# TensorE's unit loop written out, and the second tile's scores cut in two around half of the output products

## The reference, cut to what matters

```python
for i in range(DEPTH):                                # 6
    x = attn_layer(shift_tokens(x), Wqkv[i], ...) + x
    x = ffn_layer(shift_tokens(x), ...) + x

def attn_layer(x, Wqkv, qs, ksc, Wo):                 # 16 heads of 64, INNER = 1024
    q, k, v = jnp.split(x @ Wqkv, 3, -1)
    q = l2norm(q) * qs;  k = l2norm(k) * ksc          # per head
    q = q * cos * scale + rotate_half(q) * sin * scale
    k = k * cos / scale + rotate_half(k) * sin / scale
    # windows of 32 queries see their own 32 keys and the 32 before them
    attn = jax.nn.softmax(jnp.where(mask, low, q @ k.T * 8.0), -1)
    return (attn @ v) @ Wo

def ffn_layer(x, g, bln, W1, b1, W2, b2):
    xn = layernorm(x) * g + bln
    a, gate = jnp.split(xn @ W1 + b1, 2, -1)
    return a * gelu(gate) @ W2 + b2
```

## Time and profile before

| | us |
|---|---|
| median of 3 runs | 3477.61 |
| lowest, highest | 3473.73, 3481.7 |
| the profiled execution's own time | 3467.71 |
| its span | 3465.9 |
| mean granted TensorE clock | 0.979 of full |

### The profile page before, as it was taken

How to read it: one execution, slowest core, us unless ns; L and a number is a source line. 1 busy time by engine, 2 the same in 40 slices (tenths; PEclk the granted TensorE clock), 3 DMA queues, 4 the chain that set the end, 5 groups by cost and what they waited for, 6 DMA issues and landing times.

```text
span 3465.9 us, 129619 instructions
## 1 busy us (share of the span) xinstructions
PE 3224.8 (93%) x51488; PEld 2289.5 (66%) x51488; DVE 2896.2 (84%) x5656; ACT 2801.5 (81%) x5313; POOL 2685.9 (77%) x1798
## 2 busy tenths in 40 slices
PE   8999799899999899998999999999999999998996
PEld 5777466666666666675667766666766677766665
DVE  6999788788888888897779898888988788887784
ACT  5777588778888788887889888888988788887884
POOL 1001598778888889998789998889988889988883
PEclk9999899999999999999999999999999999999998
DMA  2000011111211111211112211112211112211111
GB/s 66 0 0 0 7 34 37 37 29 39 59 38 39 39 28 51 57 39 35 31 34 53 50 38 38 39 34 55 50 35 39 39 31 54 51 39 33 33 39 51
DMA packets 127341, 129.59 MB, mean 37 GB/s; under 512 B 62380, under 2 KB 75824, under 8 KB 126832
## 3 DMA queue, kind: packets, MB, share of 16 engines
q1 hardware_dynamic: 123232, 112.38, 13.3%
q10 hardware_dynamic: 3600, 9.50, 0.9%
HBM read 19.04 MB, written 2.10 MB: 6 GB/s over the span
## 4 chain that ended last, share of the span: by engine, by line
PE 75%; issue 10%; DVE 6%; POOL 5%; SPq 1%; DMA 1%; ACT 1%; DVEq 0%; POOLq 0%; ACTq 0%
PE ps L1313 23%; PE ps L1335 9%; PE ps L1328 8%; PE ps L1344 7%; PE ps L1357 7%; PE ps L1305 6%; PE ps L1367 4%; PE ps L1169 3%; POOL area L446 2%; PE ps L1161 2%; POOL AQb L453 2%; PE ps L1158 2%; DVE area L991 2%; PE ps L1181 1%; PE ps L1154 1%
## 5 line engine op out<-in xcount | busy, mean ns | idle before, releaser
L1313 PE MATMUL ps<-Wqkv,xsT 128*128 128x512 f32 x2304 | 1138.3, 617 | 9.0 <-DMA Wqkv<-ffn_Wqkv 3.4
L446 POOL TENSOR_TENSOR area<-area,tab 128x512 f32<-128x512 f32 x768 | 960.6, 1280 | 108.8 <-ACT area L634 107.7
L1313 PEld LDWEIGHTS ps<-Wqkv,xsT 128*128 128x128 f32 x2304 | 403.9, 196 | 341.1 <-issue 240.3
L468 POOL TENSOR_TENSOR area<-area,lsum 128x1024 f32<-128x1024 f32 x192 | 365.7, 1905 | 284.9 <-DVE lsum L932 284.8
L453 POOL TENSOR_TENSOR area<-area 128x1024 f32<-128x1024 f32 x192 | 452.8, 2374 | 46.8 <-DVE area L991 46.8
L634 ACT ACTIVATE area<-ps 128x512 f32<-128x512 f32 x768 | 455.1, 593 | 35.2 <-PE ps L1313 34.4
L453 POOL TENSOR_TENSOR AQb<-AQb,area 128x1024 f32<-128x1024 f32 x192 | 449.5, 2364 | 0.1
L639 ACT ACTIVATE area<-area 128x1024 f32<-128x1024 f32 x384 | 396.5, 1065 | 0.1
L1335 PE MATMUL ps<-Wo,area 128*128 128x128 f32 x3072 | 376.4, 281 | 20.9 <-issue 20.8
L1335 PEld LDWEIGHTS ps<-Wo,area 128*128 128x128 f32 x3072 | 356.4, 194 | 33.8 <-issue 25.4
L1328 PEld LDWEIGHTS ps<-BD,area 64*64 64x64 f32 x12288 | 270.0, 133 | 144.8 <-issue 133.4
(11 more groups left out here) (124 smaller groups left out, 6416.3 us busy)
## 6 DMA issues: line engine op xcount, KB each, us to landing
BD<-area SPq DMA_DIRECT2D x1440, 64.0 KB, 2.0
Wqkv<-ffn_Wqkv ACTq DMA_DIRECT2D x12, 512.0 KB, 3.9
x2s<-x2s SPq DMA_DIRECT2D x96, 56.0 KB, 2.1
Wo<-ffn_Wo SPq DMA_DIRECT2D x6, 512.0 KB, 4.9
Wqkv<-ffn_Wqkv ACTq DMA_DIRECT2D x12, 256.0 KB, 3.1
W<-ffn_W SPq DMA_DIRECT2D x6, 341.0 KB
x2s<-x2s SPq DMA_DIRECT2D x96, 7.5 KB, 2.5
x2s<-x2s SPq DMA_DIRECT2D x96, 0.2 KB, 1.9
```

The source lines that it names most:

```text
L446: pool.tensor_tensor(b4[:, :, here], q4[:, :, there], s4[:, :, here], ALU.mult).then_inc((s_bq, s_bk)[j], 1)
L468: pool.tensor_tensor(p3, p3, lsum[:, 1, :].unsqueeze(2).broadcast_to([P, HEADS, 2 * WIN]), ALU.mult).then_inc(s_pn, 1)
L1313: mm(home(kind + part), xsT[:, par, t * P:(t + 1) * P], Wqkv[:, w0:w0 + 512], start=True, stop=True).then_inc(done, 1)
```

## The change

`stack_steps_straight` calls `step` for all 99 steps with plain numbers, and TensorE alone uses it. TensorE's program then has no loop in the stack, no register instructions for its waits, and the static steps' waits in every step. The other four engines keep their loops. Second, `scores(n-1, 1)` is called in two parts: pairs 0 to 3, then `output(n-2, 0, 0)` and `output(n-2, 1, 0)`, then pairs 4 to 7, then the g = 1 products. The waits stand ahead of the first part, and `s_sc` is raised after the second.

```diff
+        def stack_steps_straight(step, lags):
+
+            for n in range(UNITS + lags):
+                u = n % SEQS
+                step(n, u, u % 2, live(n), n // SEQS)
...
-            def scores(n, t):
+            def scores(n, t, pairs=range(PAIRS)):
 
-                need_apart(pe, i_pe, s_mk, 4 * n + 2 * t + 2)
-                if isinstance(n, int):
-                    need_apart(pe, i_pe, s_te, nth(n, EVICTED, "q11" if t else "q00"))
-                for c in range(PAIRS):
+                if 0 in pairs:
+                    need_apart(pe, i_pe, s_mk, 4 * n + 2 * t + 2)
+                    if isinstance(n, int):
+                        need_apart(pe, i_pe, s_te, nth(n, EVICTED, "q11" if t else "q00"))
+                for c in pairs:
...
-                last.then_inc(s_sc, 1)
+                if PAIRS - 1 in pairs:
+                    last.then_inc(s_sc, 1)
...
                 if one:
-                    scores(n - 1, 1)
+                    scores(n - 1, 1, range(0, PAIRS // 2))
...
                     output(n - 2, 0, 0)
                     output(n - 2, 1, 0)
+                if one:
+                    scores(n - 1, 1, range(PAIRS // 2, PAIRS))
+                if two:
                     need(pe, s_oe, 4 * (n - 2) + 4)
...
-            stack_steps(pe, step, 3)
+            stack_steps_straight(step, 3)
```

More of the change, by code:

```diff
@@ L236, in upto, with live @@
             return min(n, UNITS - 1) if isinstance(n, int) else n
+        def live(n):
+            return [0 <= n - lag < UNITS for lag in range(4)]
         def stack_steps(eng, step, lags):
-            def live(n):
-                return [0 <= n - lag < UNITS for lag in range(4)]
             for L in range(DEPTH):
```

## The result

The changed kernel takes 3449.25 us (median of 5 runs, 3440.13 to 3454.12) against 3479.34 for the kernel before (5 runs, 3473.73 to 3490.37): a ratio of 0.9909, 95% interval 0.9885 to 0.9934. It is faster, by 30 us or 0.9%, where 78 us were forecast. Its profiled execution took 3448.8 us with a span of 3447.0 and a mean granted clock of 0.99.

A forecast was written before the change was run, and what follows sets the result against it. TensorE, busy 93% of the span, was taken as nearly the bound. 370.4 + 83.3 + 2795.9 (92 steps) + 32 + 4 + 101.2 + 1.4 gave a 3388 us span, 3400 us from the median; 8-in-10 range 3268 to 3450.

The forecast's parts named there:

- The loop written out: TensorE's stack: 24 jumps of about 3 us vanish; each step's TensorE work falls to 29.03 us, 92 steps 2670.8 us.
- The stops in the first scores: Instruction packet edges falling into the first scores stop TensorE in 20 steps by 1.6 us, 32 us; bounds 0 and 156.
- the price of a split step, 29.03 + 1.36: Later end of second scores idles TensorE 1.36 us beyond 29.03 of work each step; 125 us over 92 steps.
- the path to xn: Through VectorE's softmax to TensorE's transposes of xn: 1.92 later, less 0.15 and 0.41 of slack, costs 1.36 us.
- the path to "k00": Through ScalarE's copy of V01 to TensorE's last four transposes: 1.92 later, less 0.56 of slack, costs 1.36 us.
- What the split saved: Around the second scores: with eight output products spreading the burst, no stall was counted there.
- B: Rival: the full 1.92 us reaches TensorE each step, slacks being lost elsewhere; 3452 us, chance 14%.
- A: Rival: later scores cost nothing, other engines' idle time absorbing them; 3275 us, chance 12%.
- C: Rival: the new 1.36 us pause lowers the clock in every step, 135 us more; 3535 us, chance 7%.
- D: Rival: straight code stalls in every step, 72 more steps by 1.6 us; 3515 us, chance 7%.
- The signs that I named: Trace marks expected on TensorE and VectorE, such as 30.4 us steps and waits over 1 us at "k00" or xn.

The follow-up runs named there:

- whole_good: whole plus semaphore increments filling each TensorE step to 1024 instructions, packet edge 220 instructions into the step: 3250.41 us, ratio 0.9339 to the kernel before.
- whole: TensorE's loop written out as in the change, but the second scores in one piece as before: 3345.99 us, ratio 0.9619 to the kernel before.
- split_good: The changed kernel with the same filling to 1024 instructions as whole_good: 3406.94 us, ratio 0.9811 to the kernel before.
- res_first: split_good with VectorE's first residual moved ahead of a 1.2 us sum: 3404.04 us, ratio 0.9806 to the kernel before.
- three: split_good with residual ahead of a sum and layer norm ahead of a turn (VectorE), and a mask later (ScalarE): 3414.36 us, ratio 0.9835 to the kernel before.
- whole_bad: whole_good with 60 filling increments fewer in unit 0, putting the packet edge inside the first scores: 3386.3 us, ratio 0.973 to the kernel before.
- split_loop: The kernel before with its loop kept, only the second scores cut in two around eight output products: 3626.48 us, ratio 1.0417.

## Why the prediction was right in direction and wrong in size

**The loop written out: right.** The jumps' waits are gone, and the steps are alike; in whole_good, without split and stops, most lie within 0.1 to 0.4 us of the good step. The gain of writing out alone is 137 us (whole).

**The stops in the first scores: right.** Forecast 20 steps, 32 us. The trace has 13 stops in or just behind the first scores (L1364 and L1311), 23.9 us, in units 3 to 6 and 81 to 94, with a lower clock in some of them, and around the second scores a single one of 0.7 us. The filling, which removes them, gains 34 us by the ratios and 44.3 between the two profiled executions (2886.44 − 2842.16). More than the stops themselves goes with them: in seven of these steps the clock was 0.95 and TensorE busy about 31.5 us and not 29.7, some 12 us by this estimate.

Unit 83's stop in the timeline:

```profile
2958.86 0.35 PE L1364 MATMUL ps<-kT,area 64*32 64x64 f32 x16 [1.95 <-issue]
```

**The step that failed: the price of a split step, 29.03 + 1.36.** The 92 steps of the changed kernel sum to 2886.44 us where the forecast had 2795.9 + 32 + 4 = 2831.9. These 54.5 us, with 4.3 more at the stack's start, are the 59 us by which its span passed the forecast 3388. The experiments divide them:

- 21 us are the floor. Without split and stops the steps sum to 2695.91 (whole_good), against 92 x 29.03 + 4 = 2674.8: most steps carry 0.1 to 0.4 us of small waits. I had made the best two steps of the earlier trace rows the price of all.
- 21 us are the split. It costs 146.3 us over 92 steps (split_good against whole_good), 1.59 a step, where I had 125, 1.36 a step.
- 12 us are the stops, 44.3 against 32.

The split's 1.59 is near 1.36 in size but made of other things. A switch's price was not in the sum: 0.36 us a step, 33 us in all, since I had put the work down as the same, and no row of before showed a switch apart. The turns cost 1.13, but the join was another: "q01" waits for VectorE's residual. The prediction followed the path to xn and the path to "k00" and passed over this one, since in the earlier trace rows it was met: the residual ended at 2475.73, and "q01" was due at about 2476.4 (behind four of the 12 transposes of 1.51 us that start at 2475.97). Counted as the other two were, it would have given 1.92 − 0.15 − 0.7 = 1.1 us. And about 0.19 us a step stands ahead of the values (L1334 on L640: 22.4 us in 44 waits, against 4.5 in 10 in whole_good), a third join that I passed over. The three sum to 1.68; the 0.09 between that and 1.59 I have not placed. Of the two paths that I did follow, the one to "k00" would hold 0.95 a step by itself (res_first) and not 1.36, and the one to xn, moved ahead in three, gave nothing back.

**What the split saved: not in the sum.** The prediction counted no stop around the second scores with the split, and put no price on what they would cost without it; in whole they are 41 stops and 41.7 us. In medians, all stops are worth 96 us in whole (against whole_good) and 42 in the changed kernel (against split_good, 34 by the ratios), so the split removes some 54 us of stops and costs some 157: net 103 us lost.

**The rivals.** The time is that of B (3452), and B's mechanism in part: more than 1.36 reached TensorE in each step, though by switches and a further join and not by the full 1.92. A (nothing) is refuted by whole_good against split_good. C did not come: in ordinary steps the granted clock stayed at 1.00 with stops of 0.80 us. It was 0.95 in unit 83, where a stop in the first scores came on top, and 0.91 in unit 70 of split_loop. A longer stop can do it without a split, but rarely does: in whole_bad, with 63 stops of about 1.7 us, the clock was 0.90 in unit 22 and 0.95 in ten other steps. D as a rule for all straight code is refuted by whole_good and whole, but whole_bad shows that most steps can be made to stop by a shift of 60 instructions.

**The signs that I named.** No wait of 3 us ahead of the first transposes: so. Steps of 30.4 with TensorE busy 29.0: 30.9 with 29.7. A wait of over 1 us ahead of "k00" or xn: 0.80 ahead of "q01", with 0.20 behind it at "k00". VectorE waiting 2.3 us: 2.52 in the step shown, 248.9 / 102 = 2.44 in the mean.

## What to carry to other kernels

When a signal is moved later, list every instruction that waits on anything computed behind it, with its slack, and not only the two that look closest; those that were met show no wait in the profile before. Pieces of small products put between large ones are not free, even where the work is the same: ask what the switches cost before cutting a burst in two. Where a dense burst of small instructions stops on "issue" in straight code, count the instructions of a step and shift or fill them, before changing the schedule: here that was worth 96 us (whole to whole_good), and the split that was meant to dodge the same stops cost more than it saved.

## What the runs showed of the hardware

- A stop at an instruction packet's edge in straight code: 1.66 us in the mean (112.9 / 68, whole_bad) within a burst in which TensorE runs 128 products and 128 loads in 1.48 us; none with the edge 60 instructions away. The stops end 1.42 us (1.23 to 1.60, 63 stops) after an instruction packet has landed.
- Two extra switches between 64x32 score products and 128x128 output products: 0.36 us a step together, the same for four and for eight products between; about 0.24 us from scores to output products and 0.1 back, by the starts of the products.
- A wait and a taken jump behind it add up on TensorE: 0.85 us, and then about 3 us (91.6 us in 28 waits); the granted clock of the step behind was 0.91.
- A stop of 0.80 us in each of 92 steps left the granted clock at 1.00 (split_good); with a stop of 1.95 us in the first scores beside it, it was 0.95 and 31.52 us of busy time in place of 29.73 (unit 83 of the changed kernel). It is no fixed price of a stop: with one of 2.22 us beside it, the clock stayed at 1.00 in unit 81; in whole_bad a stop of 2.55 us alone gave 0.90 (unit 22), and one of 2.23 us 1.00 (unit 68).
